# Two expert layers cut into pairs of 128 rows, with later scatters and plain fp32 products in the last one

## Time and profile before

| | us |
|---|---|
| Median of 3 runs (492.86 to 499.9) | 497.24 |
| The profiled execution, its own time | 498.54 |
| Its span, first to last instruction | 496.7 |
| PE busy in the span | 389.3 |
| DVE busy | 313.0 |
| ACT busy | 243.1 |
| POOL busy | 207.1 |

### The profile page before, as it was taken

How to read it: one execution, slowest core, us unless ns; L and a number is a source line. 1 busy time by engine, 2 the same in 40 slices (tenths; PEclk the granted TensorE clock), 3 DMA queues, 4 the chain that set the end, 5 groups by cost and what they waited for, 6 DMA issues and landing times.

```text
span 496.7 us, 7564 instructions
## 1 busy us (share of the span) xinstructions
PE 389.3 (78%) x2149; PEld 309.5 (62%) x2149; DVE 313.0 (63%) x895; ACT 243.1 (49%) x544; POOL 207.1 (42%) x219
## 2 busy tenths in 40 slices
PE   8960479997887999973479799999827999798840
PEld 7950453335776874362358589878713999788830
DVE  2740254984864664544475689999867788677632
ACT  2310032422443454271338588787612899687720
POOL 4277245040000217877200010624552288788780
PEclk9985559998999899976769899999966899899985
DMA  3861015974678546345726223311016684576616
GB/s 105 213 195 51 23 63 211 353 224 161 188 258 252 185 138 207 121 163 168 295 114 237 62 59 96 109 53 59 30 44 173 189 173 80 137 161 150 159 22 234
DMA packets 66735, 73.42 MB, mean 148 GB/s; under 512 B 11941, under 2 KB 55782, under 8 KB 66182
## 3 DMA queue, kind: packets, MB, share of 16 engines
q1 hardware_dynamic: 53574, 52.64, 34.2%
q0 software_dynamic: 9952, 9.08, 9.5%
q10 hardware_dynamic: 3168, 11.22, 5.7%
HBM read 34.50 MB, written 31.42 MB: 133 GB/s over the span
## 4 chain that ended last, share of the span: by engine, by line
PE 48%; DVE 18%; issue 10%; POOL 8%; DMA 6%; another core or an unknown queue 5%; ACT 2%; SPq 1%; DVEq 0%; POOLq 0%; ACTq 0%
POOL ygat L794 7%; PE ps L1630 6%; PE ps L2015 6%; PE ps L1632 5%; PE ps L1631 5%; DVE hid_lo L1404 4%; PE ps L1812 4%; PE ps L1822 3%; DMA yd<-yr 3%; PE ps L1760 3%; PE ps L1771 3%; PE ps L1727 2%; PE ps L2017 2%; PE ps L1729 2%
## 5 line engine op out<-in xcount | busy, mean ns | idle before, releaser
L951 ACT ACTIVATE hid<-ps,cols 128x512 f32<-128x512 f32 (+3 forms) x84 | 52.0, 621 | 36.1 <-PE ps L1632 29.5
L1404 DVE TENSOR_TENSOR hid_lo<-hid,hid_hi 128x512 fp32r<-128x512 f32 (+3 forms) x84 | 48.9, 600 | 16.4 <-ACT hid_hi L955 12.4
L812 POOL DMA_INDIRECT disp<-stage,idx x32 | 33.4, 1044 | 47.1 <-DVE idx L1478 38.6
L756 POOL DMA_INDIRECT xd<-stage,idx x36 | 35.7, 992 | 31.9 <-DVE idx L1148 21.8
L794 POOL DMA_INDIRECT ygat<-yd,idxy x36 | 41.4, 1149 | 17.8 <-issue 17.8
L955 ACT ACTIVATE hid_hi<-ps,cols 128x512 fp32r<-128x512 f32 (+3 forms) x73 | 45.3, 621 | 0.0
L893 ACT ACTIVATE hid<-ps,cols 128x512 f32<-128x512 f32 x35 | 23.8, 687 | 36.8 <-PE ps L1760 22.6
L1630 PE MATMUL ps<-in_hi,wc 128*128 128x512 f32 (+3 forms) x84 | 34.5, 411 | 6.0 <-DVE in_lo L1344 6.0
L1760 PE MATMUL ps<-h_f,raw 128*128 128x512 f32 x70 | 36.9, 620 | 0.0
L853 POOL DMA_INDIRECT out_dram<-ysb,xrow_a x16 | 26.7, 1667 | 22.9 <-DVE ysb L1596 18.7
L1630 PE MATMUL ps<-hid_hi,wc 128*128 128x512 f32 (+3 forms) x84 | 32.5, 387 | 3.1 <-issue 2.3
(11 more groups left out here) (294 smaller groups left out, 1144.0 us busy)
## 6 DMA issues: line engine op xcount, KB each, us to landing
disp<-empty ACTq DMA_DIRECT2D x16, 616.5 KB
w1d<-wf SPq DMA_DIRECT2D x15, 512.0 KB
yd<-yr SPq DMA_DIRECT2D x48, 128.0 KB, 2.4
xd<-zero SPq DMA_DIRECT2D x32, 128.0 KB
g0c<-gt_d SPq DMA_DIRECT2D x8, 512.0 KB
g0a<-gt_d SPq DMA_DIRECT2D x3, 1280.0 KB
xr_a<-xd SPq DMA_DIRECT2D x24, 128.0 KB, 3.2
xr_b<-xd SPq DMA_DIRECT2D x24, 128.0 KB, 3.0
```

The source lines that it names most:

```text
L756: G.indirect_dma_start(out=xd, out_offset=bass.IndirectOffsetOnAxis(ap=idx0[:, i, k:k + 1].bitcast(U32), axis=0), in_=stage0[:, i, :], in_ ...
L812: G.indirect_dma_start(out=disp, out_offset=bass.IndirectOffsetOnAxis(ap=idx[:, i, k:k + 1].bitcast(U32), axis=0), in_=stage[:, i, :], in_ ...
L951: A.activation(hid[:, n % 4, lo:hi], src, ACT.Gelu_apprx_tanh, bias=bias).then_inc(s_hid, 1)
L1404: V.tensor_tensor(hid_lo[:, n % RING, a:b], hid[:, n % 4, a:b], hid_hi[:, n % RING, a:b].bitcast(F32), ALU.subtract).then_inc(s_lo, 1)
```

## The change

**First expert layer.** A tile now has 128 rows (`TR`), and two tiles make a pair that is transposed, copied out, loaded and stored as one turn. There are 35 tiles from the table, so 66 tiles in 33 pairs, where there were 48 turns of 256 rows. The two tiles of a pair have their own weights, so the first product and the gelu are done per tile. `NA` is 23: eight dense items are moved from behind the sparse loop to ahead of it. The 36 scatters are issued only when the recurrence has ended, and the adding of x to h is moved ahead of them on POOL. The table's values are 35 instead of 17, read by PE, POOL and SP in two calls each. POOL's copies have four places instead of two.

**Last expert layer.** Tiles have 128 rows, 8 fixed and 31 from the table, NTAU = 39, in 20 pairs. Products are plain fp32 of the unsplit values; `wf_split` and all other splitting is gone, and SP loads the weights directly. The loads of fixed pairs are 4 instead of 8; the tiles from the table have a load each, and a weight and a bias copy each, into one of four places. A tile has one accumulating scatter, tiles go by turns into `out` and `out2`, and scatter h waits for scatter h - 2 to have landed. The two tables read by SP, PE and DVE have 31 values instead of 15.

```diff
-TR = 256
+TR = 128
+PR = 2 * TR
 STR0 = N_TOK0 + TR
 M0 = N_TOK0 // TR - 1
 DYN0 = (N_TOK0 * K0 - K0) // TR
-NT0 = E0 + DYN0
+NH0 = E0 + DYN0
+assert NH0 % 2 == 0
+NT0 = NH0 // 2
 ROWS0 = E0 * STR0 + TR
+W0 = 4
+LOAD0 = 18
 XR0 = 12
-WC_AT = list(range(8, 28, 4)) + list(range(32, 47, 3))
+WC_AT = list(range(3, 33, 3))
 DENSE = [(0, q) for q in range(J0)] + [(e, SQ) for e in range(1, N0)]
 N_ITEMS0 = len(DENSE)
-NA = 15
+NA = 23
 N_A = J0 + NA
 LAG0 = 3
 NG0 = 5
+NGA = -(-NA // NG0)
 ORDER = [0, SQ] + list(range(1, SQ))
...
+TS = 128
 STATIC = EF
 DYN = NT * KF // TS - 1
 NTAU = STATIC + DYN
+NPAIR = (NTAU + 1) // 2
 RANKS = NT
+M1 = RANKS // TS - 1
 N_PIECE = RANKS // P
 AWAY = 1 << 20
 XR = 16
 KB = 1024
-WR = 4
+W1 = 4
 def build(nc, x, cond, Wx, Wh, rb, ws1, bs1, ws2, bs2, We1, Be1, We2, Be2, Wr, br,
```

POOL, the order of residual and scatter; SP, dense gates, loads and stores of the first layer:

```diff
-            pool.wait_ge(s_h, 9)
-            residual(0)
+            for q in range(SQ):
+                pool.wait_ge(s_h, 8 * q + 9)
+                residual(q)
+            pool.wait_ge(s_h, T)
             for q in range(SQ):
                 scatter0(q)
-            for q in range(1, 4):
-                if q < SQ:
-                    pool.wait_ge(s_x1, q + 1)
-                residual(q)
+            residual(SQ)
...
                 fill(e)
-            sp.wait_ge(s_hg0, NG0)
-            gates_a(2)
+            for k in range(2, NGA):
+                sp.wait_ge(s_hg0, NG0 * (k - 1))
+                gates_a(k)
...
             def load0(t):
-                at_row = (t * STR0 if t < E0 else first_of0[t - E0])
-                rows_of = xd[at_row:at_row + TR, :] if t < E0 else xd[bass.ds(at_row, TR), :]
-                sp.dma_start(xr0(t), rows0(rows_of)).then_inc(s_ld[t % XR0], 16)
+                if 2 * t + 1 < E0:
+                    two_of = xd[2 * t * STR0:(2 * t + 2) * STR0, :].rearrange("(a s) d -> s a d", a=2)
+                    sp.dma_start(xr0(t), two_of[0:TR, :, :]).then_inc(s_ld[t % XR0], 16)
+                    return
+                for a in range(2):
+                    h = 2 * t + a
+                    at_row = h * STR0 if h < E0 else first_of0[h - E0]
+                    rows_of = xd[at_row:at_row + TR, :] if h < E0 else xd[bass.ds(at_row, TR), :]
+                    sp.dma_start(xr0(t)[:, a, :], rows_of).then_inc(s_ld[t % XR0], 16)
             def store0(t):
                 sp.wait_ge(s_yo, t + 1)
-                sp.dma_start(rows0(yd[t * TR:t * TR + TR, :]), yr[:, t % 4, :, :]).then_inc(s_yst[t % 4], 16)
+                sp.dma_start(yd[t * PR:t * PR + PR, :].rearrange("(a p) d -> p a d", a=2), yr[:, t % 4, :, :]
+                             ).then_inc(s_yst[t % 4], 16)
...
             sp.dma_start(rawc1[:, 1:NC_, 1, :], ew1.rearrange("e k f -> k e f")).then_inc(s_wc, 16)
             sp.wait_ge(s_tab, 3)
-            first_of0 = multi(tab0[0:1, 0, :], mybir.EngineType.SP, E0 * STR0)
+            first_of0 = (multi(tab0[0:1, 0, 0:LOAD0], mybir.EngineType.SP, E0 * STR0)
+                         + multi(tab0[0:1, 0, LOAD0:DYN0], mybir.EngineType.SP, E0 * STR0))
             for t in range(NT0):
```

PE, the first product of the first layer:

```diff
@@ -1803,22 +1766,27 @@
                 pe.wait_ge(s_xlo, t + 1)
                 if t >= 2:
                     pe.wait_ge(s_thi, t - 1)
-                if t < E0:
-                    wts = raw1[:, t + 1, :]
-                else:
-                    j = t - E0
-                    pe.wait_ge(s_w1d0, 2 * j + 2)
-                    wts = w1d0[:, j % 2, :]
-                M.matmul(bank(6 + t % 2)[:, 0:TR], wts, xs0[:, t % 3, :], start=True, stop=True).then_inc(s_m1, 1)
+                for a in range(2):
+                    h = 2 * t + a
+                    if h < E0:
+                        wts = raw1[:, h + 1, :]
+                    else:
+                        j = h - E0
+                        pe.wait_ge(s_w1d0, 2 * j + 2)
+                        wts = w1d0[:, j % W0, :]
+                    op = M.matmul(bank(6 + t % 2)[:, a * TR:(a + 1) * TR], wts, xs0[:, t % 3, a * TR:(a + 1) * TR],
+                                  start=True, stop=True, skip_group_check=True)
+                op.then_inc(s_m1, 1)
             def out0(t):
```

SP in the last layer, its loads and weights:

```diff
-            for k in range(WR, 2 * EF):
-                sp.wait_ge(s_wfl, k - WR + 1)
-                wf_load(k)
...
+                if 2 * t < STATIC:
+                    sp.dma_start(xrow(t), disp_rs[0:TS, 2 * t:2 * t + 2, :]).then_inc(s_ld[t], 16)
+                    return
+                for a, h in two(t):
+                    sp.dma_start(xrow(t)[:, a, :], disp[bass.ds(first_of[h - STATIC], TS, step=S1), :]
+                                 ).then_inc(s_ld[t], 16)
+            def weights(j):
                 e = expert_of[j]
-                if j >= 2:
-                    sp.wait_ge(s_m1, NT0 + 2 * (t - 2) + 2)
-                    sp.wait_ge(s_rb, t - 1)
+                t = (STATIC + j) // 2
+                if j >= W1:
+                    sp.wait_ge(s_m1, NT0 + 2 * (t - W1 // 2) + 2)
+                    sp.wait_ge(s_rb, t - W1 // 2 + 1)
                 else:
-                    sp.wait_ge(s_wfl, 2 * EF)
-                sp.dma_start(w1d[:, j % 2, :, :].bitcast(F32),
-                             wf1[:, bass.ds(e, 1), :, :].rearrange("p o a b -> p (o a) b").bitcast(F32)
-                             ).then_inc(s_w1d[j % 2], 16)
-                sp.dma_start(b1d[:, j % 2, :], cols[:, bass.ds(e * FC + R_BF, FC)]).then_inc(s_w1d[j % 2], 16)
+                    sp.wait_ge(s_wf1, 16)
+                sp.dma_start(w1d[:, j % W1, :], wf1[:, bass.ds(e, 1), :].rearrange("p o f -> p (o f)")
+                             ).then_inc(s_w1d[j % W1], 16)
+                sp.dma_start(b1d[:, j % W1, :], cols[:, bass.ds(e * FC + R_BF, FC)]).then_inc(s_w1d[j % W1], 16)
             sp.wait_ge(s_disp, 16 * (T0 * K0 + 4 * K0 + TILES * KF))
-            for t in range(STATIC):
+            for t in range(STATIC // 2):
                 load(t)
...
+            expert_of = multi(tab[0:1, 1, 0:W1], mybir.EngineType.SP, EF - 1)
+            for j in range(W1):
+                weights(j)
+            first_of = multi(tab[0:1, 0, 0:DYN], mybir.EngineType.SP, (RANKS - TS) * S1 + EF)
+            for t in range(STATIC // 2, NPAIR):
                 load(t)
-            for t in range(STATIC + 2, NTAU):
-                weights(t)
+            expert_of += multi(tab[0:1, 1, W1:DYN], mybir.EngineType.SP, EF - 1)
+            for j in range(W1, DYN):
+                weights(j)
```

POOL in the last layer, and PE's first product there:

```diff
-            for t in range(NTAU):
-                pool.wait_ge(s_yev, 2 * t + 2)
-                if t == 0:
+            for h in range(NTAU):
+                pool.wait_ge(s_yev, h + 1)
+                if h == 0:
                     for k in range(2):
                         pool.wait_ge(s_base[k], 64)
-                if t == 1:
+                if h == 1:
                     pool.wait_ge(s_base2, 16 * 8)
-                if t >= 2:
-                    added(pool, t - 2)
-                for a in range(2):
-                    G.indirect_dma_start(
-                        out=(out_rows, out2)[t % 2],
-                        out_offset=bass.IndirectOffsetOnAxis(ap=xrow(t)[:, a, D:D + 1].bitcast(U32), axis=0),
-                        in_=ysb[:, t % 3, a, :], in_offset=None, bounds_check=NT - 1, oob_is_err=False,
-                        compute_op=ALU.add).then_inc(s_sa[t % 2], 16)
+                if h >= 2:
+                    added(pool, h - 2)
+                G.indirect_dma_start(
+                    out=(out_rows, out2)[h % 2],
+                    out_offset=bass.IndirectOffsetOnAxis(ap=xrow(h // 2)[:, h % 2, D:D + 1].bitcast(U32), axis=0),
+                    in_=ysb[:, h // 2 % 3, h % 2, :], in_offset=None, bounds_check=NT - 1, oob_is_err=False,
+                    compute_op=ALU.add).then_inc(s_sa[h % 2], 16)
...
-                for h in range(2):
-                    if t >= 2:
-                        pe.wait_ge((s_ra, s_rb)[h], t - 1)
-                    for f in (2 * h, 2 * h + 1):
-                        wts = wf1[:, t, :, :] if t < STATIC else w1d[:, (t - STATIC) % 2, :, :]
-                        op = mm3(bank(2 + 2 * (t % 2) + h)[:, TS * (f % 2):TS * (f % 2) + TS],
-                                 (wts[:, 0, f * P:(f + 1) * P], wts[:, 1, f * P:(f + 1) * P]),
-                                 (xs_hl[:, t % 3, 0, :], xs_hl[:, t % 3, 1, :]))
-                    op.then_inc(s_m1, 1)
+                pe.wait_ge(s_wf1, 16)
+                for _, h in two(t):
+                    if h >= STATIC:
+                        j = h - STATIC
+                        pe.wait_ge(s_w1d[j % W1], 32 * (j // W1 + 1))
+                for f in range(FC):
+                    if t >= 2 and f % 2 == 0:
+                        pe.wait_ge((s_ra, s_rb)[f // 2], t - 1)
+                    for a, h in two(t):
+                        wts = wf1[:, h, :] if h < STATIC else w1d[:, (h - STATIC) % W1, :]
```

(20 more changed lines are left out.)

365 lines of the change are left out of this document (152 added, 213 removed).

## The result

The changed kernel took 503.75 us (median of 4 runs, 501.13 to 507.89), the kernel before 495.91 (4 runs, 492.86 to 499.90) on the same chip. The ratio is 1.0216, 95% interval 1.0157 to 1.0276: slower beyond the noise, by 1.6 to 2.8%. The profiled execution took 502.63 us, its span is 500.9. The forecast, 459 us and faster, was wrong. What happened has the mechanism of rival E; that it also meets E's 503 us is luck, as the last column of the table shows: E has 43 us of stall and all other terms as forecast, and the rows miss the forecast by 23.7, 5.3, 7.7 and 5.4 us.

What follows compares the result with a forecast made beforehand. Bounds were taken as the recurrence stalled by scatters, PE's sparse loop with stalls, POOL's gather, and POOL's last-layer scatters. Terms summed to -37.9 from 498.54, 460.6, and 459 us for the median, 1.3 lower; range 445 to 483.

Steps and rivals of the forecast that it cites:

- rival E: Dense items: the stall moves there with the scatters, 38 us lost and 5 for the clock, 503 us; chance 0.05.
- Recurrence, -27.9: Recurrence: with the scatters gone from it, ten tanh steps take 1.05 us each instead of 38.45 in all, -27.9 us.
- Do the scatters hide?: Ahead of the sparse loop: 36 scatters take 46 us, landing and loads end near 93; dense items cover them by about 8.
- Before the loop, -2, +13.8, +2.8, +3.1: Before the sparse loop: full clock -2, eight more dense items +13.8, table operations +2.8, table reading +3.1; start at 104.3 us.
- Sparse loop, -19.2: Sparse loop: 33 turns instead of 48, about 49 us with SP, POOL and stalls, against 68.2: -19.2 us.
- Gather, -1.5: Gather on POOL's queue: 36 DMAs as before, some steps faster with half the dense items beside them gone, -1.5 us.
- Middle layer, -5: Middle layer: DVE, taken as busiest, loses ten splits, then PE and ACT set the pace, -5 us.
- Last layer, -2: Last layer: 39 scatters at 2.15 us, -7; start -1; stalls from SP's order +6; together -2 us.

Runs made afterwards that it cites:

- after: The changed kernel as it is, its profiled execution, against the kernel before on the same chip: median 503.75 us, ratio 1.0216; profiled execution 502.63 us.
- after_again: The changed kernel, to the byte, run again on another chip, where the kernel before took 468.04 us: 472.09 us, ratio 1.0148.
- last_order: The changed kernel with only SP's order in the last layer changed (12 table loads, expert numbers, then weights with the other loads between): 494.47 us, ratio 0.9924 to before.
- before_late: The kernel before with its scatters moved after the recurrence and the residual additions ahead of them: 498.84 us against 497.87.
- before_again: The kernel before, unchanged, run again to get it without the stall: 495.09 us against 497.77.
- paced runs: Early scatters with zeros written before each, additions between quarters: changed kernel with 512 or 128 zeros, 499.24 and 488.82 us; kernel before with 256, 493.99 us.
- free_order: Changed kernel with early scatters, 384 zeros before each in four buffers so POOL's queue works ahead, and SP's other last-layer order: 469.56 us, ratio 1.0059 to before.
- early_paced: Changed kernel with scatters starting in the recurrence and 512 zeros written by POOL before each but the first: 514.84 us, ratio 1.0287 to before.
- early_spaced: Changed kernel with scatters starting in the recurrence and 1536 zeros written by POOL before each but the first: 543.17 us, ratio 1.0912 to before.
- last_dve: Changed kernel with the last layer's weights and biases copied by DVE instead of SP's DMAs: 496.68 us, ratio 0.9873 to before.

## Why the prediction was wrong, point by point

- **Recurrence, -27.9.** Measured -29.6. Right, in cause too: the runs with early, spaced and late scatters show that the stall there was the scatters'.
- **"Do the scatters hide?"** This is the step that failed: the overlap of scatters and dense items. I took 46 us of scatters beside dense items as free, put the stall's cost there at nothing, and gave as the reason PE's busy time beside twelve of them. From 46.23 us until 88.20 five items start in after, 22 in after_again, which lacks only the stall; it reaches the first product 24.5 us earlier. Rival E had the mechanism and got 0.05 of the chance. Its size was wrong: 43 us against 24.5, and the 13.1 us beside the gather (below) it did not have. The counter-argument against E was a row that is true for twelve scatters, whose pause is made good, and was carried over to 36.
- **Before the loop, -2, +13.8, +2.8, +3.1.** Table reading 6.35 against 2.91, +3.4; an item 1.72, eight of them 13.8. The other two were not measured apart. The sum is right where nothing stalls: 103.55 against 104.3.
- **Sparse loop, -19.2.** Measured -13.9. 54.8 us, within the bounds of 41 and 60. While SP loads table tiles, one store follows another in 1.6 us (14 turns from 143.4 to 169.5, less one pause of 3.8): SP's two loads bind in full, 1.5 us as worked out, 7 us in all, of which I had charged 4. And two waits in the chain alone, 5.09 us for a store and 4.80 for a weight load, exceed the 7 us that I kept for all stalls. (The terms of the sum are 36.6 + 4 + 2 + 7 = 49.6, taken as 49; this moves nothing.)
- **Gather, -1.5.** POOL's steps were 1.31 us from the start; its last DMA ended 6.3 us earlier than before, at 233.0, or 50.1 us behind the last store instead of 56.0. Nothing came of it in after: the chain has the same unnamed waits beside the gather, in the middle layer's first units, until 236. In after_again the gather itself is in the chain, and its landing, and the whole stretch to the last layer is 13.1 us shorter. So a second piece of stall, which no rival had, hid what the gather gained. First after, then after_again:

```profile
215.68 4.73 issue
...
221.11 4.36 issue
...
226.63 6.53 issue
...
234.43 2.30 another core or an unknown queue
```
```profile
209.74 6.31 DMA ygat<-yd,idxy
```

- **Middle layer, -5.** Measured 0 together with the gather. The windows of before and of after, in this order, show DVE 8.3 us less busy, and PE as before. PE was the bound, in the row that I read as DVE's: 9.96 beside 9.79.

```profile
250.00:376.00 126.00, 107.73 (x553) 88.48 (x552) 101.60 (x296) 83.46 (x154) 35.21 (x33) 0.91 0.28 86
```
```profile
250.00:376.00 126.00, 107.27 (x553) 88.71 (x552) 93.27 (x274) 83.69 (x155) 34.73 (x33) 0.91 0.28 91
```

- **Last layer, -2.** Measured +4.4. The period of 4.4 us per pair is right (4.41 from 428.1 to 467.8). The stalls weren't 6 us but 10 (93.7 us from the first to the last scatter, less 38 x 2.2), 6.5 of them between pairs 4 and 5. last_order takes 5.3 us back.

What stays open: why only some chips stall, what is held up there, why the gather stalls in one place and not in another, and whether the rate decides or POOL's working ahead, since the kernels that could tell fell on chips without the stall.

## What to carry to other kernels

Read progress on the consumer: a stretch is undisturbed only if the engine that waits for PE keeps its step, whatever PE's busy time says. A pause that is made good from results in hand says how deep the buffer is, not that the work is free; before three times as much is put there, compare the length of the new stretch with the one that was measured. Don't take a total that comes out right for a rival that was right: put its terms beside the rows. And run both kernels on several chips: here a change of 2% stood beside a difference of 6% between chips.

## What the runs showed of the hardware

- Back-to-back indirect DMAs of POOL (0.98 us and 0.30 between) hold up PE, ACT and SP in the traces of the result, of the experiments on the chip of before_late and last_order and of before_again. On the chip of after_again they don't. Two more chips are placed by the time of before alone: 495 us on that of the paced runs, 468 on that of free_order.
- With a gap after each (one in 2.27 us or slower, on a chip where the stall is traced) they hold up nothing that the traces show: tanh ends at 36, and 25 fills of SP take 15.4 us (early_paced) and 15.66 (early_spaced). On the chip of the paced runs 128 zeros on one partition, 0.19 us, with a wait for them, were enough (one in 2.0 us).
- Twelve in a row beside dense items cost 0.7 us or nothing in the end, 36 cost 24.5.
- The stall's length varies between executions: the last dense item starts at 112.9, 117.7 and 119.4 us in three kernels that are alike up to there (last_order, after, last_dve).
- The Trainium skill, "SBUF — State Buffer", section "Who interferes with whom", says that PE and ACT never wait on anyone. In after_again the trace agrees, with steps of 1.72 us beside the scatters. In after ACT is idle for 12.01 us before 72.84; the profile names no releaser, so it can't be said whether this is a wait of the kind that the section, which is about ports, speaks of.
